# Delta rule: small products side by side on halves of the array that do not meet, finer pieces of the solve, and a new order of the step on all engines

## The reference, cut to what matters

```python
q = q / (norm(q) + EPS); k = k / (norm(k) + EPS)
alpha = sigmoid(h @ alpha_w + alpha_b); beta = sigmoid(h @ beta_w + beta_b)
def step(s, inp):                      # for each token, and each head
    qt, kt, vt, at, bt = inp
    s = s * at[..., None]
    u = einsum('bhd,bhdv->bhv', kt, s)
    s = s + bt * (kt[..., None] * (vt - u)[..., None, :])
    out = einsum('bhdv,bhd->bhv', s, qt)
    return (s, out)
y = y * rsqrt(mean(y * y) + EPS) * head_norm_w
y = x + (y @ out_w) * gate
```

## Time and profile before

| | |
|---|---|
| median of 3 runs | 6315.5 us (6315.34 to 6328.09) |
| the profiled execution, its own time | 6313.83 us |
| its span | 6312.0 us |
| PE busy in the span | 5286.4 us (84%) |
| POOL busy | 2502.6 us (40%) |
| DVE busy | 3573.1 us (57%) |
| ACT busy | 2311.8 us (37%) |
| granted clock, mean of the span | 0.917 |

### The profile page before, as it was taken

One profiled execution on the slowest core, in us unless ns is written; L12 is line 12 of the kernel. 1 busy time (PEld: TensorE's weight loads), 2 busy tenths in 40 slices (PEclk: granted clock), 3 DMA queues, 4 the chain that ended last, 5 costly groups with the idle time before them and its releaser, 6 DMA issues. The chain is left out here.

```text
span 6312.0 us, 183438 instructions
## 1 busy us (share of the span) xinstructions
PE 5286.4 (84%) x72156; PEld 3821.8 (61%) x72156; DVE 3573.1 (57%) x9528; ACT 2311.8 (37%) x4102; POOL 2502.6 (40%) x2792
## 2 busy tenths in 40 slices
PE   4569767888866888988988889888679999787998
PEld 3434344555544777777777777777446666576776
DVE  4531256778775655655655565556545455675333
ACT  3432234666642333333333333333213333111333
POOL 1210013444444666666666666666410000574000
PEclk7779978999987999999999999999889999898999
DMA  0000001000000000000000000000010000000000
GB/s 18 0 19 0 2 0 41 0 0 0 0 1 14 11 11 11 11 11 11 11 13 11 11 11 11 11 11 11 9 41 0 0 0 0 4 1 28 0 0 13
DMA packets 29529, 57.57 MB, mean 9 GB/s; under 512 B 7312, under 2 KB 14240, under 8 KB 28704
## 3 DMA queue, kind: packets, MB, share of 16 engines
q1 hardware_dynamic: 28960, 48.86, 2.5%
HBM read 46.75 MB, written 2.10 MB: 8 GB/s over the span
## 5 line engine op out<-in xcount | busy, mean ns | idle before, releaser
L617 PEld LDWEIGHTS psum<-m_wd,m_h 128*128 128x128 f32 x6144 | 810.3, 193 | 484.7 <-issue 483.6
L617 PE MATMUL psum<-m_wd,m_h 128*128 128x128 f32 x6144 | 823.7, 277 | 92.3 <-remote 65.5
L2077 POOL TENSOR_TENSOR e_kd<-e_kd,e_tail 128x512 f32<-128x512 f32 x325 | 368.7, 1134 | 566.6 <-PE psum L2184 553.3
L607 PE MATMUL psum<-xT,m_wa 128*128 (+1 forms) x1032 | 549.4, 615 | 8.5 <-remote 8.5
L607 PE MATMUL psum<-xT,m_wb 128*128 (+1 forms) x1032 | 537.3, 603 | 0.0
L784 DVE SCALAR_TENSOR_TENSOR m_acc<-psum,m_combine,m_acc 128x128 f32<-128x128 f32 x1440 | 403.3, 342 | 224.9 <-PE psum L617 210.0
L544 POOL TENSOR_TENSOR m_h<-m_td,m_tb 128x512 f32<-128x512 f32 x258 | 328.6, 1274 | 480.1 <-DVE m_tb L812 480.1
L2214 PE MATMUL psum<-e_T,e_N 64*64 64x32 f32 x10400 | 403.2, 231 | 66.1 <-remote 65.2
L2214 PEld LDWEIGHTS psum<-e_T,e_N 64*64 64x64 f32 x10400 | 367.0, 147 | 112.8 <-issue 110.0
L2184 PE MATMUL psum<-e_kd,e_k 64*64 64x64 f32 x10400 | 415.4, 235 | 1.2 <-issue 0.8
L143 POOL TENSOR_SCALAR m_post_rstd<-m_post_mv 128x4 f32<-128x4 f32 x27 | 6.2, 228 | 991.0 <-DVE m_post_mv L133 991.0
(11 more groups left out here) (432 smaller groups left out, 11999.7 us busy)
## 6 DMA issues: line engine op xcount, KB each, us to landing
e_w<-in_e_w SPq DMA_DIRECT2D x66, 321.0 KB, 2.9
m_wa<-in_m_wa SPq DMA_DIRECT2D x12, 512.0 KB, 6.7
m_wd<-in_m_wd SPq DMA_DIRECT2D x12, 512.0 KB, 8.0
m_wb<-in_m_wb SPq DMA_DIRECT2D x8, 512.0 KB, 8.4
f_h<-in_f_h SPq DMA_DIRECT2D x2, 1024.0 KB
out<-x SPq DMA_DIRECT2D x1, 2048.0 KB, 8.7
f_w<-in_f_w SPq DMA_DIRECT2D x3, 256.0 KB
g_w<-in_g_w SPq DMA_DIRECT2D x3, 256.0 KB
```

Source lines behind the costliest of these rows:

```text
L607: pe.matmul(c.ps[i][:], w[q][:, j, :], xb, start=True, stop=True).then_inc(a_ready[i], 1)
L617: r = pe.matmul(c.ps[4 + e % 2][:, t * P:(t + 1) * P], h[:, u % DEPTH, t * P:(t + 1) * P], wd[u // UQ][:, u % UQ, :], start=(m == 0 and t ...
L2077: return g.tensor_tensor(both_odd(dst[:], m), both_odd(src[:], m), gate.unsqueeze(1).broadcast_to((P, 2, nb, m)), ALU.mult)
```

## The change

It does this, all of it inside `stage_delta`:

1. `keys_by_tokens` goes. Its products stand one by one between those of the last `t_step(5)`, and write to the other column half (`half(1 - h)`). `t_step(5)` now waits for `ks_done` at its start.
2. `diagonal` and `gram(1)` become `gram_and_diagonal`, chunk by chunk in turn; the diagonal's products write to the other column half. It stands behind `solve(0)`, where `gram(1)` stood ahead of it.
3. Since head h now lies in the other half, ACT's copy to `ket` is two of 64x512, moved from a round's end behind the copies of `k`, `ZX` and `kd`; DVE's write of the diagonal is two of 64x512 (`own_tokens`). The copy to `k` now waits for `ke_ps`.
4. `project_qk`, `square_sums` and `project_gates` are cut in two. `project_q` stands ahead of `t_step(1)`, `project_k` behind it. `state_and_output(3)` moves ahead of `key_norms`.
5. POOL: the power for the scales moves from ahead of the last `carry_k` to behind the last `carry_kq`, still ahead of the copy to `tH`; the copy to `owp` moves ahead of `hidden`.
6. ACT: two copies of U move up by one place. DVE: the copy to `TX` moves ahead of a write to `AT`; `masked(3)`, `transposed(1)` and `residual(2)` now stand ahead of the copy of Z at level 2; smaller moves of the same sort follow.

```diff
@@ POOL
+                g.tensor_copy(owp[:], ow[:, bass.ds(((i + LAST - 1) % LAST) // B, 1), :].rearrange("p o d -> p (o d)"))
                 g.wait_ge(hs_free, 1)
                 g.sem_clear(hs_free)
                 hidden(i + 1)
...
                 gated_keys().then_inc(kd_ready, 1)
-                g.wait_ge(su_ready, 1)
-                g.sem_clear(su_ready)
-                flat_su = su[:].rearrange("p t h -> p (t h)")
-                g.tensor_tensor(flat_su, flat_su, c.mhalf[:, 0:2 * TB], ALU.pow).then_inc(rs_ready, 1)
                 g.wait_ge(gr_ps, 1)
                 g.sem_clear(gr_ps)
                 g.sem_inc(gx_fwd, 1)
                 carry_k(LEVELS, k).then_inc(ks_done, 1)
                 carry_kq(LEVELS, kdH, kd).then_inc(kdh_done, 1)
+                g.wait_ge(su_ready, 1)
+                g.sem_clear(su_ready)
+                flat_su = su[:].rearrange("p t h -> p (t h)")
+                g.tensor_tensor(flat_su, flat_su, c.mhalf[:, 0:2 * TB], ALU.pow).then_inc(rs_ready, 1)
                 g.tensor_copy(tH[:], tails(LEVELS + 1)).then_inc(kd_free, 1)
@@ PE
+            def gram_and_diagonal():
...
+                for u in range(NC):
+                    r = gram_chunk(1, k, kd, u)
+                    if u + 1 == NC:
+                        r.then_inc(gr_ps, 1)
+                    for h in range(2):
+                        r = pe.matmul(c.psum[half(1 - h), X_, chunk(u)], kn[half(h), chunk(u)], kqn[half(h), 1, chunk(u)],
+                                      start=True, stop=True)
+                r.then_inc(d_ps, 1)
@@ PE, t_step
+                if l + 1 == LEVELS:
+                    pe.wait_ge(ks_done, 1)
+                    pe.sem_clear(ks_done)
...
-                r.then_inc(t_ps, 1)
+                    if u + 1 == NC:
+                        r.then_inc(t_ps, 1)
+                    if l + 1 == LEVELS:
+                        for h in range(2):
+                            r = pe.matmul(c.psum[half(1 - h), X_, chunk(u)], k[half(h), chunk(u)], eye[half(h), :],
+                                          start=True, stop=True)
+                if l + 1 == LEVELS:
+                    r.then_inc(ke_ps, 1)
@@ PE, step
                 cross_t()
-                diagonal()
...
-                gram(1, k, kd, gr_free, gr_ps)
                 solve(0)
+                gram_and_diagonal()
...
-                t_step(1)
                 pe.wait_ge(out_free, 1)
                 pe.sem_clear(out_free)
-                project_qk()
+                project_q()
+                t_step(1)
+                project_k()
...
+                state_and_output(3)
                 key_norms()
-                state_and_output(3)
                 project_v()
...
                 t_step(5)
-                keys_by_tokens()
@@ ACT
+                a.wait_ge(ke_ps, 1)
+                a.sem_clear(ke_ps)
                 a.activation(odd(k[:], 1), odd(kn[:], 1), ACT.Copy).then_inc(k_free, 1)
...
                 a.activation(both_even(kd[:], 1), both_even(kdn[:], 1), ACT.Copy).then_inc(even_ready, 1)
+                ket_copies()
                 u_copy()
@@ DVE
+                own_tokens()
+                rest()
                 state(1)
+                rest = masked(3, gr_fwd)
+                transposed(1)
+                residual(2)
                 rest()
-                transposed(1)
                 z_copy()
-                masked(3, gr_fwd)()
-                residual(2)
                 sums_in()
```

More of the change, by code:

```diff
@@ L2169, in _ @@
             pe.sem_clear(consts_ready)
[L2171 to L2179, removed]
             def gram_chunk(l, keys, gated, u):
@@ L2308, in from_state, with project_q @@
                               start=True, stop=False, skip_group_check=True)
-            def project_qk():
+            def project_q():
                 pe.wait_ge(w_ready, 16)
@@ L2315, in project_qk, with project_k, squares_of, sums_q @@
                 pe.sem_clear(hs_ready)
[L2316 to L2320, removed]
+                pe.matmul(c.ps[Q_][:], W[:, 0:P], hs[:], start=True, stop=True)
+            def project_k():
+                pe.matmul(c.ps[K_][:], W[:, P:2 * P], hs[:], start=True, stop=True).then_inc(qk_ps, 1)
+            def squares_of(n):
+                for t in range(TB):
+                    at = 2 * (n * TB + t)
+                    r = pe.matmul(c.ps[X_][:, at:at + 2], sq[:, n, block(t)], hm[:], start=True, stop=True)
+                return r
+            def sums_q():
                 pe.wait_ge(sq_ready, 1)
                 pe.sem_clear(sq_ready)
[L2324 to L2334, removed]
+                squares_of(0)
+            def sums_k():
+                squares_of(1).then_inc(ss_ps, 1)
+            def project_alpha():
+                pe.matmul(c.ps[Q_][:], W[:, 2 * P:3 * P], hs[:], start=True, stop=True)
+            def project_beta():
+                pe.matmul(c.ps[K_][:], W[:, 3 * P:4 * P], hs[:], start=True, stop=True).then_inc(ab_ps, 1)
             def key_norms():
@@ L2370, in output @@
                 r.then_inc(out_ps, 1)
[L2372 to L2379, removed]
-            project_qk()
-            square_sums()
-            project_gates()
+            project_q()
+            project_k()
+            sums_q()
+            sums_k()
+            project_alpha()
+            project_beta()
             key_norms()
@@ L2486, in z_copy, with ket_copies @@
                 a.activation(flat(Z[half(0)]), c.psum[half(1), Z_, 0:NC * HC], ACT.Copy).then_inc(z_ready[0], 1)
+            def ket_copies():
+                for h in range(2):
+                    r = a.activation(flat(ket[half(h)]), c.psum[half(1 - h), X_, :], ACT.Copy)
+                r.then_inc(ket_ready, 1)
             def u_copy():
@@ L2542, in _ @@
                 t_copy(5)
-                a.wait_ge(ke_ps, 1)
-                a.sem_clear(ke_ps)
-                a.activation(flat(ket), c.ps[X_][:], ACT.Copy).then_inc(ket_ready, 1)
             a.wait_ge(kd_free, 1)
             a.sem_clear(kd_free)
+            a.wait_ge(ke_ps, 1)
+            a.sem_clear(ke_ps)
         @block_.vector
@@ L2581, in masked, with own_tokens @@
                 return lambda: v.copy_predicated(cols(AT[:]), wide(lowi[:, l, :]), gr[:, :, 1]).then_inc(gr_free, 1)
+            def own_tokens():
+                for h in range(2):
+                    r = v.copy_predicated(chunks(AT[half(h)]), eyei[half(h)].unsqueeze(1).broadcast_to((DH, NC, CH)),
+                                          chunks(c.psum[half(1 - h), X_, :]))
+                ch.link(r)
             def z_copy():
```

41 lines of the change are left out of this document (22 added, 19 removed).

## The result

The changed kernel takes 6394.1 us (median of 4 runs, 6381.1 to 6413.0), the kernel before beside it 6320.2 us (6315.3 to 6328.1). The ratio is 1.0118, with a 95% interval of 1.010 to 1.0136: slower by 1.2%. The forecast was 6313 us with a range of 6235 to 6370; the time lies 24 us above its upper end.

A forecast was written before the change was run, and what follows sets the result against it. The prediction took PE and the chain through ACT and POOL, in a dead heat, as the bound. 65 x (+0.1 front + 0.3 middle - 0.3 clock) - 8 for loop jumps = -1.5 us: 6313 us, range 6235 to 6370.

The forecast's parts named there:

- PE and POOL in a dead heat: Ahead of gram(1): PE and POOL's chain finish together, so the 2.06 us taken off PE become idle time.
- side by side is free while it runs: keys_by_tokens and the diagonal cost nothing beside t_step and gram; PE has 2.06 us less a round.
- POOL's end of the round: The power ahead of the copy to tH delays ACT's copy to k to 2590.4; front +0.1 us a round.
- The first rival: PE was the bound: 2.44 us a round come off, 6155 us; some such gain has chance 0.35.
- halving the projections, -0.4 us: Ahead of t_step(1): project_q covers PE's wait for Z, saving 0.4 us a round up to z_and_gram(2).
- level 2, +0.7 us: DVE's new order makes Z late, so t_step(2) starts 0.7 us later; with the 0.4 gain, middle +0.3.
- the clock: Half clock behind the square sums and t_step(2) comes again; longer rounds regain 0.3 of 0.4 us under it.
- the clock falls in the front as well: Half clock behind PE's idle time in the front costs 2 us in each round it hits; chance 0.17.
- four of ten: The share of rounds with half clock in the front at which the clock rival costs 52 us, 6365 us.
- The price of 1.6 us for a stretch: A half-clock stretch costs 1.6 us where PE is the bound: a round of 37.5 us against 35.9.
- the loop's jumps, -8 us: After five loop jumps POOL catches up while PE idles, so 1.6 us is saved each time, -8 us.
- no change: The forecast itself, 6295 to 6335 us, chance 0.42.

The follow-up runs named there:

- a6: The changed kernel with both side-by-side groups taken apart, their products in turn in the same places: 6387 us, ratio 1.0107.
- a7: The changed kernel with POOL's power last, DVE's level 2 as before, 64-column square-sums mask, and the diagonal in turn behind gram(1): 6211 us, ratio 0.9827.
- b7: The kernel before with only the products side by side, gram_and_diagonal behind solve(0), and POOL's power behind the copy to tH: 6320 us, ratio 1.0002.
- a1: The changed kernel with POOL's power for the scales behind the copy to tH: 6366 us, ratio 1.0066.
- a3: The changed kernel with POOL's power behind the copy to tH and DVE's level 2 in the order of before: 6290 us, ratio 0.9953.
- b2: The kernel before with DVE's level 2 in the changed kernel's order, a write to AT also moved: 6389 us, ratio 1.0108.
- a2: The changed kernel with DVE's level 2 in the order of before, the copy of Z ahead of masked(3): 6314 us, ratio 0.9984.
- b5: The kernel before with DVE's level 2 in the changed kernel's order and the square-sums mask 64 columns wide: 6333 us, ratio 1.0022.
- a4: The changed kernel with an unused 256-column product ahead of cross_t and another ahead of solve(0): 6382 us, ratio 1.0097.
- a8: The changed kernel with power last, level 2 as before, 64-column square-sums mask, and unused 128-column products ahead of cross_t and solve(0): 6194 us, ratio 0.9807.
- b1: The kernel before with the square-sums mask 64 columns wide in place of 2: 6240 us, ratio 0.9870.
- a9: The changed kernel with the square-sums mask 64 columns wide and nothing else: 6321 us, ratio 0.9997.

## Why the prediction was wrong

**Right: PE and POOL in a dead heat.** The 2.06 us taken off PE bought nothing: they became idle time ahead of `cross_t`, `solve(0)` and S, at the forecast places and sizes. Over the whole full-clock round (2212.88 to 2248.53, `gram(0)` to `gram(0)`) PE is busy for 30.2 us, 2 less than before, as forecast. a6 and a7 give PE 2 and 1 us back at no cost, and b7 puts the pairs' value at zero with POOL's power out of the way.

**Right: side by side is free while it runs.** The 64 records take 1.0 us. The rule that different row tiles can't access the same PSUM bank at once (the Trainium skill, TensorEngine Tiling (Array Packing), "Restrictions and Gotchas") doesn't show here: both row halves write bank `X_`, and no time is lost. What the forecast may have missed is the supply of instructions, below.

**Right: POOL's end of the round.** The copy to `k` waits for the power, the front of round 2 is 0.2 us longer where 0.1 was forecast, and a1 shows the price of that place, 28 us. The first rival, PE's gain in full, needed this chain to be early. Even then only 0 (b7) to some 30 us (a3) came.

**Not shown: halving the projections, -0.4 us.** The wait for Z ahead of `t_step(1)` is gone in the changed kernel and in a3, and is 23.3 us in 63 rounds in b7, which has all of a3 but this and the smaller moves. But a3 is some 30 us faster than b7, and its shortest full-clock round is 0.95 us shorter, twice the term. The smaller moves, which the sum put at nothing, may have a part in it: the wait ahead of `solve(0)` for `TX`, whose copy moved ahead of a write to `AT`, is 71.8 us in 65 in b7 and 47.0 in a3. Neither was run by itself.

**Right at full clock, wrong in its cost: level 2, +0.7 us.** The wait is 44.4 / 65 = 0.68 us. But the order costs 73 us (b2), 80 (a2) or 90 (b5), not 45, because the rounds that wait there also run more at half clock: 399 us against 287 (b2), 232 against 61 (b5).

**The step that failed: the clock.** "A round that has more waits can lose a part of the longer round again under it: I take 0.3 of the 0.4 us back." The sum took half clock as a fixed amount, part of which new waits would hide. The reverse holds: the new waits brought more of it (b2 and b5 at level 2; a4 and a8 in the front, by filling them). Half clock rose from 287 to 444 us. At the 0.35 us per us of b1, the 157 more cost an estimated 55 us. The rival "the clock falls in the front as well" (0.17) named the mechanism and one of the two places; it came in 21 rounds of 65 where I priced "four of ten". The other place is the stretch behind the square sums: onsets between 18 and 27 us into a round rose from 46 to 62. I had no rival in which the wait that I had forecast at level 2 did the same. The price of 1.6 us for a stretch was off as well: it came from two single rounds. In the trace of before, leaving out rounds with a jump of the loop, the 10 rounds without half clock take 36.4 us on average and the 35 with one stretch 37.5, 1.1 apart.

**Wrong: the loop's jumps, -8 us.** The five idle times in the earlier trace rows are the loop's first entry (1.5 us) and four jumps back (3.3 to 4.4 us), since 65 rounds are five passes of 13; the text ahead and the prediction count five jumps. The eight rounds on both sides of the four jumps took 336.3 us before and 342.4 after, from `gram(0)` to `gram(0)`: 6 us more, not 8 less.

**Missing: stalls of the issue.** They rose from 19 to 47 us, 28 us more. With the clock's 55 that is 83 us; the stage lost 78. The split is an estimate; that half clock costs time is shown by b1 and a9, which take much of it away; that the stalls do, only by their rows. a6 halves them, but with other work added, so their cost wasn't measured apart.

So "no change" was right for the round at full clock and for no other: the changed kernel has one such round of 64. From `output` to `output` that round takes 37.44 us with one stall of 1.38 us in it, so 36.1 without it, as forecast (36.1 to 36.4), if the stall costs its whole length. From `gram(0)` to `gram(0)` the stall lies ahead of it and it takes 35.65 us, with 0.78 us of idle time ahead of `cross_t` in place of 1.20; with these 0.42 put back it is 36.1 again.

## What to carry to other kernels

Before adding a wait on the busiest engine, look at what the clock does around it: here a wait of 0.7 us a round cost 1.6 to 2.1 times its length, with narrow square sums (73 and 80 us in 65 rounds) and with wide ones (90). Where the clock's rows show half clock at one recurring place, widen or fill what PE streams there first; here one mask made 62 columns wider gained 1.3% on the kernel before. And work taken off an engine in a dead heat should be left where it was until the other chain is shorter.

## What the runs showed of the hardware

- **Columns nobody reads paid for themselves.** 8 products a round of 128x64 in place of 128x2 (16 records) took the stage's half clock from 287 to 61 us, and the shortest full-clock round stayed at 35.9 us.
- **PE's stalls keep step with the transfers of instructions.** In the trace the 16 KB transfers of the instruction queue q8 (taken for PE's) last about 1.1 us and start some 5.7 us apart. The three stalls inside `t_step(5)` of rounds 3, 4 and 5 end 2.7, 2.3 and 2.2 us after the start of one. Of all 28 stalls over 0.8 us in the changed stage 26 end 2.2 to 2.8 us after such a start and two 3.3 to 3.4; all 11 of the stage before end 2.2 to 2.6 us after one. They mostly come back at the same places of the 13 unrolled rounds (in `t_step(5)`: 3 to 5, 11 and 12 of each 13). That PE outran its instructions there is the reading that fits. The Trainium skill (Runtime: NRT & Kernel Launch, "Instruction fetch mechanics") says that PE's instructions are refilled in blocks of 16 KiB and that crossing a block is mostly hidden. The size agrees with the trace, the hiding doesn't here, if this is the cause. The cause is argued from these times; no run changed the supply alone.
